# Alignment directives behind the projections of the last stage of a one-core, four-layer kernel

## What is computed

```python
for i in range(DEPTH):          # DEPTH = 6, HEADS = 16, DIM_HEAD = 64, WINDOW = 32
    x = attn_layer(shift_tokens(x), Wqkv[i], q_scale[i], k_scale[i], Wo[i]) + x
    x = ffn_layer(shift_tokens(x), ln_g[i], ln_b[i], W1[i], b1[i], W2[i], b2[i]) + x

def attn_layer(x, Wqkv, qs, ksc, Wo):
    q, k, v = jnp.split(x @ Wqkv, 3, -1)            # then 16 heads of 64
    q, k = l2norm(q) * qs, l2norm(k) * ksc          # then both are rotated, with a scale
    out = local_attention(q, k, v)                  # windows of 32 tokens, keys of 2 windows
    return out @ Wo

def ffn_layer(x, g, bln, W1, b1, W2, b2):
    a, gate = jnp.split((layernorm(x) * g + bln) @ W1 + b1, 2, -1)
    return a * jax.nn.gelu(gate, approximate=False) @ W2 + b2
```

## Time and profile before

| | |
|---|---|
| median of the runs | 4664.67 us (4663.52 to 4666.86) |
| the profiled execution, first to last instruction | 4655.4 us |
| last stage | from about 1450 us to the end |
| PE busy over the span | 4360.4 us (94%), 56640 matmuls and 56640 weight loads |
| DVE, ACT, POOL busy | 3703.2 us (80%), 3238.4 us (70%), 3648.6 us (78%) |
| granted TensorE clock, mean | 0.984 |

### The profile page before, as it was taken

One profiled execution on the slowest core, in us unless ns is written; L12 is line 12 of the kernel. 1 busy time (PEld: TensorE's weight loads), 2 busy tenths in 40 slices (PEclk: granted clock), 3 DMA queues, 4 the chain that ended last, 5 costly groups with the idle time before them and its releaser, 6 DMA issues.

```text
span 4655.4 us, 137933 instructions
## 1 busy us (share of the span) xinstructions
PE 4360.4 (94%) x56640; PEld 2936.9 (63%) x56640; DVE 3703.2 (80%) x5128; ACT 3238.4 (70%) x6002; POOL 3648.6 (78%) x1951
## 2 busy tenths in 40 slices
PE   7889899978887999999999999999999999999998
PEld 4556688854443666666666666666666666666665
DVE  6874476759997888888888788888888788878885
ACT  4666655657774777777777777777777777777775
POOL 2223344469997999988999899989999898989993
PEclk9999999989998999999999999999999999999999
DMA  2000000023331222322233322323223222322222
GB/s 81 2 2 2 2 1 1 1 110 146 146 146 57 67 63 61 80 65 66 58 70 74 71 63 61 79 66 69 58 67 76 69 64 60 78 68 66 59 68 53
DMA packets 164376, 290.47 MB, mean 62 GB/s; under 512 B 44063, under 2 KB 61350, under 8 KB 159654
## 3 DMA queue, kind: packets, MB, share of 16 engines
q1 hardware_dynamic: 162310, 281.40, 23.2%
q10 hardware_dynamic: 1440, 0.24, 0.0%
HBM read 90.16 MB, written 2.62 MB: 20 GB/s over the span
## 4 chain that ended last, share of the span: by engine, by line
PE 57%; issue 4%; DVE 4%; DMA 2%; ACT 1%; SPq 1%; POOL 0%; DVEq 0%; ACTq 0%
PE ps L2626 19%; PE ps L2682 7%; PE ps L2639 7%; PE ps L2694 7%; PE ps L2655 5%; PE ps L2668 3%; PE ps L2720 3%; PE ps L2736 3%; PE ps L2727 3%; DMA L3f_vw<-L3f_v 2%; DVE L3f_ss L3019 1%; PE ps L2701 1%; PE ps L2707 1%; DVE L3f_raw L3036 1%; SPq L2472 1%
## 5 line engine op out<-in xcount | busy, mean ns | idle before, releaser
L3219 POOL TENSOR_TENSOR L3f_t<-L3f_raw,L3f_rot 128x1024 f32<-128x1024 f32 x384 | 1085.3, 2826 | 246.4 <-DVE L3f_raw L3036 242.8
L2626 PE MATMUL ps<-L3f_wqkv,all_z 128*128 128x512 f32 x2304 | 1154.1, 607 | 11.2 <-DVE L3f_raw L3036 8.8
L3236 POOL TENSOR_TENSOR L3f_raw<-L3f_raw,L3f_t 128x1024 f32<-128x1024 f32 x384 | 911.9, 2375 | 7.5
L3228 POOL TENSOR_TENSOR L3f_raw<-L3f_raw,L3f_rot 128x1024 f32<-128x1024 f32 x384 | 909.0, 2367 | 7.5
L2835 ACT ACTIVATE L3f_sqr<-ps 128x512 f32<-128x512 f32 x768 | 453.1, 595 | 295.8 <-PE ps L2626 292.4
L3036 DVE TENSOR_TENSOR L3f_raw<-ps,L3f_ri 128x512 f32<-128x512 f32 x768 | 498.7, 686 | 163.5 <-ACT L3f_ri L2845 154.4
L3019 DVE TENSOR_REDUCE L3f_ss<-L3f_sqr 128x8 f32<-128x512 f32 x768 | 515.6, 679 | 115.6 <-ACT L3f_sqr L2835 112.3
L2639 PEld LDWEIGHTS ps<-all_ident,L3f_raw 128*128 128x128 f32 x3072 | 363.3, 141 | 307.8 <-issue 270.3
L2626 PEld LDWEIGHTS ps<-L3f_wqkv,all_z 128*128 128x128 f32 x2304 | 395.8, 192 | 234.8 <-issue 180.2
L2639 PE MATMUL ps<-all_ident,L3f_raw 128*128 128x128 f32 x3072 | 474.5, 277 | 9.4 <-POOL L3f_raw L3236 3.7
L2682 PEld LDWEIGHTS ps<-L3f_pT,L3f_vw 128*64 128x64 f32 x12288 | 375.3, 138 | 97.0 <-issue 78.6
(11 more groups left out here) (332 smaller groups left out, 8632.4 us busy)
## 6 DMA issues: line engine op xcount, KB each, us to landing
L3f_vw<-L3f_v SPq DMA_DIRECT2D x1344, 128.0 KB, 2.4
L3a_Bs<-L3a_rows SPq DMA_DIRECT2D x16, 2048.0 KB, 7.1
L3a_Cs<-L3a_rows SPq DMA_DIRECT2D x16, 2048.0 KB, 11.7
L3f_vw<-L3f_v SPq DMA_DIRECT2D x192, 64.0 KB
L3f_wqkv<-in_L_ffn_Wqkv SPq DMA_DIRECT2D x24, 256.0 KB, 4.3
L3f_wqkv<-in_L_ffn_Wqkv SPq DMA_DIRECT2D x6, 512.0 KB, 4.2
L3f_wo<-in_L_ffn_Wo SPq DMA_DIRECT2D x48, 64.0 KB, 2.4
out<-all_x SPq DMA_DIRECT2D x8, 256.0 KB, 3.2
```

The lines of the kernel that those rows point to most:

```text
L2626: p.matmul(PS[:, j % 3, :], Z[:, u % NSEQ, t * P:t * P + P], w, start=True, stop=True).then_inc(proj.sem)
L3219: g.tensor_tensor(t.rearrange("p h (b e) -> p h b e", b=2), r.rearrange("p h (b e) -> p h b e", b=2)[:, :, ::-1, :], w[:, 1, :].rearrange( ...
L3228: g.tensor_tensor(r, r, w[:, 0, :].unsqueeze(1).broadcast_to((P, H, HD)), ALU.mult).then_inc(cosined.sem)
L3236: g.tensor_tensor(r, r, t, ALU.add).then_inc(rotated.sem)
```

## The change

Behind each projection from unit 4 on a directive is put into PE's stream. It asks the loader that the next instruction has a given place in a block of 256 instructions, `PLACE[x][u % 2]`, to be reached with at most 16 filler instructions (NOPs). There is one place for each of the twelve projections of an even and of an odd unit. No matmul, wait or order is altered, and no other engine's stream.

```diff
@@ -2447,6 +2447,9 @@
         halves = ((slice(0, HD), 0), (slice(HD, P), 1))
         NSMALL, NSCALES = 3 + 6, 6
         FB = (6, 7, 3)
+        BLOCK = 256
+        PLACE = {"q0a": (166, 46), "q0b": (45, 69), "k0a": (102, 89), "k0b": (122, 126), "v0a": (134, 160), "v0b": (169, 178),
+                 "q1a": (176, 185), "q1b": (65, 192), "k1a": (99, 208), "k1b": (106, 107), "v1a": (114, 115), "v1b": (35, 159)}
 
         got_c, got_m, zeroed, made, got_v, got_wo, got_w1, got_w2, got_small, got_scales, rot_in = self.signals(
@@ -2624,6 +2627,8 @@
                     if u % NSEQ == 0 and t == 0:
                         p.wait_ge(*got_qk[c].all(l))
                 p.matmul(PS[:, j % 3, :], Z[:, u % NSEQ, t * P:t * P + P], w, start=True, stop=True).then_inc(proj.sem)
+                if u >= 4:
+                    p.addr_align(BLOCK, offset=PLACE[x][u % 2], max_nops=16)
 
             def turn_qk(u, t, g):
                 if not 0 <= u < N:
```

## The result

The changed kernel takes 4616.4 us (median of 4 runs, 4615.3 to 4630.0) against 4664.1 us; the ratio is 0.9914, 95% interval 0.99 to 0.9929. The prediction said 4634.7 us and a range of 4627 to 4666. The direction and the place of the gain were right, and its size was too small: 48 us by these medians instead of 30, outside the range. By the ratio and its interval the gain is 40 us (33 to 47). On another chip the same kernel took 4621.1 us against 4656.1, 35 us less (ratio 0.992, 0.9897 to 0.9943; experiment 10). Single runs of the kernel before spread from 4641 to 4678 us over the chips used here.

What follows compares the result with a forecast made beforehand. TensorE was taken as the bound, idle 2.5% of a plain stretch. Span 4655.4 - 31 (waits) + 1 (first directive) = 4625.4 us, fillers and extra blocks 0; with 9.3 around the span 4634.7 us, range 4627 to 4666.

Steps and rivals of the forecast that it cites:

- what comes back: TensorE's issue waits, before scores and a projection, total 33.9 us; removing them returns 28 to 34 us, taken as 31.
- 34 at most by the waits themselves: Upper bound of the gain: the issue waits of TensorE, 33.9 us together, return no more than their own length.
- That blocks of 256 are the cause, and the wait sits near the end of a run of scores: TensorE's instructions come in 256-blocks; waits above 0.5 us end at boundaries in or just behind a score run's last 36 matmuls.
- The share of 0.83: Over 15 rounds with issue waits only, 16.0 of 19.2 us of waiting lengthens the round; applied to 33.9 us: 28.
- has nothing to do with the change: TensorE's wait for the output projection's weights, 17.6 us, was claimed unrelated to the change and expected to stay.
- 9.3 us lie around the span: Outside the profiled span of 4655.4 us, 9.3 us up to the median of 4664.67, added to the forecast span.
- The fillers cost nothing: Behind projections, 3600 fillers of at most 51 ns lie under the projection's second pass: 0 us; uncovered, 184 us.
- The first directive: At q0a of unit 4 the gap of some 194 slots exceeds 16: bounds 0 and 9.9 us, taken as 1.
- Rival (a): Two new boundary places, in values and scores, end short blocks and could wait, giving 23 us back: 4657 us; chance 0.06.
- Rival (b): Block crossing was hidden anyway; the 24 waits are of another make and stay: 4664.7 us; chance 0.05.
- Rival (c): Counted slots are shifted against fetched blocks; boundaries stand near score runs' ends each round, costing 87 us: 4721 us; chance 0.08.
- Rival (d): Fillers behind the projections are not covered, slower from 9 ns each, 4818 us if wholly bare; chance 0.04.

Runs made afterwards that it cites:

- experiment 10: The changed kernel run again unaltered, on another chip: 4621.1 us against 4656.1 us for the kernel before.
- experiment 1: The changed kernel with every asked place 110 slots lower, about as many fillers: 4658.1 us, ratio 0.9993 to the kernel before.
- experiment 2: The changed kernel with asked places moving 79 slots a round, so twice the fillers and drifting boundaries: 4658.9 us, ratio 1.0002 to the kernel before.
- the pair with the early load: Kernel before and changed kernel, both with Wo's load issued behind the eighth of SyncE's sixteen value transfers instead of the last: 4636.0 and 4599.6 us.
- experiments 2 and 9: Experiment 2, and the changed kernel with directives behind every third projection only, eight a round, 8 to 11 fillers each: 4618.8 us.
- experiment 6: The changed kernel with one directive a round, behind q0a of the even unit, spending all 79 fillers there: 4846.8 us, ratio 1.0404 to the kernel before.

## Why the prediction was right in kind and wrong in size

The step that failed is the term "what comes back", 31 us with a bound of "34 at most by the waits themselves". In its place 46.4 us came off the 45 rounds compared: some 25 by the waits for instructions, less what small waits took back, 6.6 by the wait for Wo, and 15 by PE's busy time, 9 to 11 of them at half clock. The last two had been put at nothing.

*That blocks of 256 are the cause, and the wait sits near the end of a run of scores:* right. Of the 24 waits 23 went; experiment 1 brings back waits of 53.6 us by the place alone, and experiment 2 brings them back by drift. That none of the 24 lay ahead of the first directive was wrong: the one at 1553.4 does.

*What comes back of the 33.9 us:* I took 31. By the rows 29.5 us of waits went (34.4 with a half microsecond before L2639, against 4.9), and 4.8 us came back as small waits for VectorE (10.6 us before the change, 15.4 after). So 24.7 us are left, 6 less than I took. That is why a round with a wait was less than the wait longer: in the kernel before such a small wait comes in 19 of the 22 rounds without a wait for issue, and in 5 of the 23 with one. The share of 0.83 was too high for these waits alone: in the 13 rounds that hold waits for issue and none of any other kind over 0.15 us, 10.6 of 14.6 us show up, which is 0.73 and gives 24.7 us of the 33.9. Fifteen rounds that are 16.0 us over come out only if the round from 2067.0 to 2134.6 is taken in, which holds a small wait for VectorE and a stretch at half clock.

*What was missing:* "34 at most by the waits themselves" took a wait to cost its own length or less. Two terms were left out. Behind some of the waits PE runs at half clock: 9 to 11 us over the rounds. I had read the mean clock of 0.99 and said that it was no subject; stretches of 0.50 are found by the same view in smaller windows, and that round from 2067.0, with a wait for issue of 1.85 us and the small one of 0.44, was 3.80 us over 63.79. And the fetches, moving with the drift, lengthened SyncE's chain in front of Wo (the reading above): 6.6 us of waits, 5.3 by experiment 10. I had written that the wait for Wo "has nothing to do with the change". The two are not apart, for seven of the nine half-clock stretches that the kernel before had are behind Wo or the residual. In the pair with the early load, where no wait for Wo is left and six stretches at half clock between 1550 us and the end of the rounds (four of them behind waits for instructions) become one, the directives bring 36 us.

*"9.3 us lie around the span":* wrong. The changed kernel's profiled execution has a span of 4614.0 us at a time of 4615.3. The profiled execution of the kernel before was some 8 us quicker than its median, within the spread of single runs. Between the two profiled executions lie 41.4 us, not 48: 46.4 in the rounds, 1.5 lost ahead of them and 3.5 behind, where the changed kernel has more of its last stretch at half clock. With 1.3 us around the span instead of 9.3 the sum would have given 4626.7 us, and the lower bound 4619; 4616.4 lies below that too.

*The fillers cost nothing:* right by experiments 2 and 9, with a wrong price. I bounded one by a wait's 51 ns; it is 76 ns in a heap. Uncovered, the 3600 would be 274 us and not 184, and experiment 6 paid 230 over the changed kernel.

*The first directive:* one jump of 2.2 us in the sequencer (1565.8), not fillers; I took 1 us. Just behind it PE waits 0.17 and 1.47 us for issue where the kernel before has no such waits, so 1.6 us is the better price. It lies ahead of the compared rounds.

*Rival (a), tight places:* it shows, but small: 3.3 us in five waits before the values, four of them (3.1 us) with 19 of the 64 matmuls left, which is the place named (90 slots in); the 1.47 us behind the first directive are one of these. *Rival (b), nothing to gain,* and with it the sentence of the Trainium skill ("Runtime: NRT & Kernel Launch", instruction fetch mechanics) that the crossing is mostly hidden: the trace agrees for the other blocks, and differs for these, whose removal took away 29.5 us of waits. *Rival (c), a wrong place:* not the case, and its price was set too high: three bad places cost 42 us in experiment 1, where 87 us were put down for one or two. *Rival (d):* see the fillers.

What stays open: why one block at the same place comes in time and another does not (the two limits of 3.3 and 6.5 us), which waits have a stretch at half clock behind them, and the remaining 4 to 6 us of PE's busy time that the half clock doesn't account for.

## What to carry to other kernels

Where the trace shows short waits of TensorE for nothing in a stream that is written out, count the instructions between them; if the count is a multiple of the fetch block, keep the boundaries out of the densest code, with fillers in small portions behind long matmuls. Look behind each wait of some 2 us for what the clock takes afterwards (1.7 us in some places here, nothing in others), and ask which transfers share their time with the fetches, since a fixed place fixes these too. Before trusting a difference between a profiled span and a median, look at how far single runs spread.

## What was not expected of the hardware

- A filler of the sequencer is recorded with 13 ns and takes 76 ns (128 in 9.7 us).
- A directive whose gap is over its limit became one jump, recorded with 2215 ns here and with 1405 and 2752 ns in experiments 2 and 9.
- With a fetch of 16 KB under way, the step of a chain of 128 KB transfers takes 3.1 us on the average instead of 2.4.
- Blocks at a fixed bad place are not late in every round: 53.6 us in 59 waits over 46 rounds with three bad places each. Half clock came behind a wait of 1.85 us and not behind one of 2.33.
